# Attention scores in three fp32r passes, with ScalarE taking each head's exponentials and sums from PSUM

## The reference

```
h   = layer_norm(x);  qh = h @ wq + bq
kh  = ctx @ wk + bk, with one bias key appended;  vh = ctx @ wv + bv, with one bias value appended
w   = softmax(qh . kh / sqrt(128))          # 64 + 1 keys
x   = x + (w @ vh) @ wo + bo
```

## Time and profile before

| | |
|---|---|
| median of 3 runs | 1015.79 us (1015.21 to 1018.17) |
| profiled execution | 1017.42 us, span 1015.6 us, mean granted PE clock 0.982 |
| PE | 922.9 us busy, 91% of the span |
| PEld | 772.6 us, 76% |
| DVE | 615.3 us, 61% |
| ACT | 532.7 us, 52% |
| POOL | 485.1 us, 48% |
| chain that ended last | PE 74%, DVE 14%, ACT 5%, issue 4%, POOL 2% |

### The profile page before, as it was taken

One profiled execution on the slowest core, in us unless ns is written; L12 is line 12 of the kernel. 1 busy time (PEld: TensorE's weight loads), 2 busy tenths in 40 slices (PEclk: granted clock), 3 DMA queues, 4 the chain that ended last, 5 costly groups with the idle time before them and its releaser, 6 DMA issues.

```text
span 1015.6 us, 16288 instructions
## 1 busy us (share of the span) xinstructions
PE 922.9 (91%) x5784; PEld 772.6 (76%) x5784; DVE 615.3 (61%) x1380; ACT 532.7 (52%) x1300; POOL 485.1 (48%) x509
## 2 busy tenths in 40 slices
PE   5899989889998999989899899899998989989798
PEld 3677777789895678956689698799975679756698
DVE  2566758541778857789631465333779857788440
ACT  3777767654664326633455343664663336632662
POOL 2645657365453424545458144083544325455373
PEclk8999999999999999999999998899999999999999
DMA  9100000000362003310000200020460005200000
GB/s 343 42 1 2 2 1 2 1 2 1 125 217 85 1 1 125 126 63 1 1 21 2 83 2 1 2 93 22 152 253 1 1 22 164 65 1 0 2 11 32
DMA packets 15027, 52.49 MB, mean 52 GB/s; under 512 B 1507, under 2 KB 4067, under 8 KB 13796
## 3 DMA queue, kind: packets, MB, share of 16 engines
q1 hardware_dynamic: 14948, 51.46, 14.6%
HBM read 50.41 MB, written 1.05 MB: 51 GB/s over the span
## 4 chain that ended last, share of the span: by engine, by line
PE 74%; DVE 14%; ACT 5%; issue 4%; POOL 2%; DMA 0%; SPq 0%; DVEq 0%; ACTq 0%; POOLq 0%
PE ps L918 7%; PE ps L894 7%; PE ps L821 5%; PE ps L823 5%; PE ps L861 5%; PE ps L850 4%; PE ps L729 4%; PE ps L649 3%; PE ps L650 3%; PE ps L651 3%; PE ps L716 3%; PE ps L630 3%; PE ps L631 3%; PE ps L632 3%; PE ps L705 2%
## 5 line engine op out<-in xcount | busy, mean ns | idle before, releaser
L894 PE MATMUL ps<-arena,hT 128*128 128x512 f32 x256 | 120.0, 613 | 19.8 <-ACT hT L1247 19.8
L918 PE MATMUL ps<-arena,pT_all 128*128 128x256 f32 x512 | 116.4, 380 | 7.3 <-ACT pT_all L1306 5.9
L493 POOL TENSOR_TENSOR arena<-arena,rinv 128x640 f32<-128x640 f32 x64 | 80.5, 1258 | 83.9 <-DVE rinv L1447 83.9
L518 POOL TENSOR_TENSOR prob<-prob,rinv 128x512 f32<-128x512 f32 x32 | 49.5, 1548 | 133.8 <-DVE rinv L1643 133.8
L918 PEld LDWEIGHTS ps<-arena,pT_all 128*128 128x128 f32 x512 | 94.8, 190 | 20.6 <-ACT pT_all L1306 6.8
L485 POOL TENSOR_TENSOR rstd<-var,neg_half 128x1 f32<-128x1 f32 (+1 forms) x56 | 35.6, 635 | 154.9 <-DVE var L1462 154.9
L1313 ACT ACTIVATE prob<-prob 128x512 f32<-128x512 f32 x32 | 20.2, 631 | 162.0 <-DVE prob L1631 162.0
L894 PEld LDWEIGHTS ps<-arena,hT 128*128 128x128 f32 x256 | 48.6, 194 | 72.9 <-issue 48.2
L1199 ACT ACTIVATE arena_r<-ps,cols 128x256 fp32r<-128x256 f32 x128 | 66.6, 520 | 61.3 <-PE ps L632 61.3
L537 POOL TENSOR_TENSOR arena_r<-arena,arena_r 128x512 fp32r<-128x512 f32 x64 | 83.9, 1331 | 13.1 <-ACT arena L1200 13.1
L461 POOL TENSOR_TENSOR vacc<-vacc,vpart 128x256 f32<-128x256 f32 x60 | 44.1, 736 | 89.9 <-ACT vpart L1282 89.6
(11 more groups left out here) (164 smaller groups left out, 2451.5 us busy)
## 6 DMA issues: line engine op xcount, KB each, us to landing
ring<-in_heads_dram SPq DMA_DIRECT2D x64, 512.5 KB, 3.4
w<-in_w_dram SPq DMA_DIRECT2D x8, 1024.0 KB, 7.2
x<-in_x_dram SPq DMA_DIRECT2D x1, 1024.0 KB, 10.3
lnb<-in_lnb_dram SPq DMA_DIRECT2D x4, 256.0 KB, 8.8
ring<-in_wp_dram SPq DMA_DIRECT2D x1, 1024.0 KB, 5.3
out_dram<-x SPq DMA_DIRECT2D x4, 256.0 KB, 2.2
arena<-in_kinT_dram SPq DMA_DIRECT2D x1, 960.0 KB, 7.6
brow<-in_brow_dram SPq DMA_DIRECT2D x1, 768.0 KB, 11.5
```

Source lines behind the costliest of these rows:

```text
L493: g.tensor_tensor(w, w, rinv[:, n % 2, 0:2].unsqueeze(2).broadcast_to([P, 2, KEYS0]), ALU.mult)\
L894: last = mm(ps[:, half, :], hT[:, k, d, 0:P], A[:, d, b // 2, cols_of, sl, :].rearrange("p r s k -> p r (s k)"), start=(d == 0), stop=(d = ...
L918: last = mm(ps[:, 6, 0:D], pT[:, k, c, :], VW[:, b, c, :], start=(c == 0), stop=(c == PAIRS - 1))
```

## The change

In the wide attentions:

- Scores take three fp32r passes: twelve matmuls of 512 columns instead of four in fp32. The low part of A, `AL`, is made by DVE for each head in keys; the low part of h, `hL`, by DVE (`low`) for each tile. The score banks alternate, (0, 1) for even tiles and (2, 5) for odd ones.
- DVE only takes the maxima and scales them by -1/sqrt(128) (`largest`). ACT then makes, for each head by itself, exp(scale * score + neg) straight from PSUM into `prob`, with the sum of the 64 values as accumulator output (`exps`): sixteen ACTIVATEs of 128x64 a tile in place of two of 128x512. DVE's subtractions and sums go. What remains on DVE (bias key, reciprocal, normalisation of the second half) is `finish`.
- All of VW is copied by ACT.
- z, spread and power run one tile (z) and two tiles (spread, power) further ahead. constant_row moves ahead of the first scores. The MLP weights are split in tiles 4 to 7 only, the high parts by ACT, since `AL` of the first two batches lies in their place.
- Some tensor_scalar operations become tensor_tensor or scalar_tensor_tensor with a broadcast operand; memory is laid out anew; mask2 and kvd are made later; some MLP steps change place in their streams.

```diff
@@ TensorE, keys
                     if n >= 2:
-                        pe.wait_ge(a_act, n - 1)
+                        pe.wait_ge(a_low, n - 1)
...
-                    if h == 0:
+                    if h == 1:
                         turn_z(0, seq * TILES, bank=6)
+                    elif h == 2:
+                        turn_z(1, seq * TILES + 1)
@@ TensorE, tokens
                 def scores(g):
                     n, k, b = base + g, g % 2, g // 2
-                    pe.wait_ge(h_ready, n + 1)
-                    if g >= 1:
-                        pe.wait_ge(s_used, n)
+                    pe.wait_ge(hq_ready, TILES * a + g + 1)
+                    if g >= 2:
+                        pe.wait_ge(e_ready, n - 1)
                     sl = slice(2 * (b % 2), 2 * (b % 2) + 2)
                     for half in range(2):
+                        o = ps[:, SCORES[k][half], :]
                         cols_of = slice(4 * half, 4 * half + 4)
                         for d in range(DH):
-                            last = mm(ps[:, half, :], hT[:, k, d, 0:P],
-                                      A[:, d, b // 2, cols_of, sl, :].rearrange("p r s k -> p r (s k)"),
-                                      start=(d == 0), stop=(d == 1))
+                            aH = A[:, d, b // 2, cols_of, sl, :].rearrange("p r s k -> p r (s k)")
+                            aL = AL[b // 2][:, d, cols_of, sl, :].rearrange("p r s k -> p r (s k)")
+                            mm(o, hH[:, k, d, 0:P], aH, start=(d == 0), stop=False)
+                            mm(o, hH[:, k, d, 0:P], aL, start=False, stop=False)
+                            last = mm(o, hL[:, k, d, 0:P], aH, start=False, stop=(d == 1))
                         last.then_inc(s_half if half == 0 else s_ps, 1)
...
+                constant_row()
+                pe.wait_ge(a_low, H * (a + 1))
                 for i in range(TILES):
                     scores(i)
-                    if i == 0:
-                        constant_row()
-                    else:
+                    if i >= 1:
                         turn_p(i - 1)
-                    if i + 1 < TILES:
-                        turn_z(i + 1, base + i + 1)
-                    if a % 2 == 1 and i == TILES - 2:
+                    if i + 2 < TILES:
+                        pe.wait_ge(hq_ready, TILES * a + i + 2)
+                        turn_z(i + 2, base + i + 2)
+                    if a % 2 == 1 and i == TILES - 1:
+                        pe.wait_ge(hq_ready, TILES * (a + 1))
                         turn_m(a, 0)
-                    if i >= 2:
+                    if 2 <= i < TILES - 1:
                         output(i - 2)
-                if a % 2 == 1:
-                    pe.wait_ge(s_used, base + TILES)
+                if a % 2 == 0:
+                    output(TILES - 3)
+                    heads_kv(a + 1, 0)
+                    heads_kv(a + 1, 1)
+                    output(TILES - 2)
+                    turn_p(TILES - 1)
+                    output(TILES - 1)
+                else:
+                    output(TILES - 3)
                     up(a, 0, range(0, 4))
                     turn_m(a, 1)
-                output(TILES - 2)
-                if a % 2 == 0:
-                    pe.wait_ge(s_used, base + TILES)
-                    heads_kv(a + 1, 0)
-                    heads_kv(a + 1, 1)
-                else:
+                    output(TILES - 2)
+                    turn_p(TILES - 1)
                     up(a, 0, range(4, 6))
-                turn_p(TILES - 1)
-                output(TILES - 1)
-                if a % 2 == 1:
+                    output(TILES - 1)
                     up(a, 0, range(6, FT))
@@ ScalarE, keys
+                        a_(VW[0:C, h % 2:B:2, h // 2, :], ps[0:C, 4 + k, :].rearrange("p (g n) -> p g n", g=2), ACT.Copy)
                         a_(VW[C:P, 1 - h % 2:B:2, h // 2, :], ps[C:P, 4 + k, :].rearrange("p (g n) -> p g n", g=2),
                            ACT.Copy).then_inc(vw_act, 1)
@@ ScalarE, tokens
+                def exps(g, half):
+
+                    k = g % 2
+                    for h in range(half * H // 2, (half + 1) * H // 2):
+                        at = h % (H // 2) * C
+                        last = a_(prob[:, k, h * C:(h + 1) * C], ps[:, SCORES[k][half], at:at + C], ACT.Exp,
+                                  bias=neg[:, k, h:h + 1], scale=scale, accum_out=sm[:, k, h:h + 1])
+                    return last
+
                 for g in range(TILES):
                     n, k = base + g, g % 2
-                    act.wait_ge(sub_half, 8 * a + g + 1)
-                    a_(prob[:, k, 0:HALF], prob[:, k, 0:HALF], ACT.Exp, scale=scale).then_inc(e_half, 1)
+                    act.wait_ge(neg_first, 8 * a + g + 1)
+                    exps(g, 0)
                     if g >= 1:
                         turned_p(g - 1)
-                    act.wait_ge(s_used, n + 1)
-                    a_(prob[:, k, H * C:PN], mx2[:, k, :], ACT.Exp, scale=-scale)
-                    a_(prob[:, k, HALF:H * C], prob[:, k, HALF:H * C], ACT.Exp, scale=scale).then_inc(e_ready, 1)
-                    if g + 1 < TILES:
-                        plus_one(base + g + 1)
-                    if a % 2 == 1 and g == TILES - 2:
+                    act.wait_ge(neg_ready, 8 * a + g + 1)
+                    a_(prob[:, k, H * C:PN], neg[:, k, :], ACT.Exp)
+                    exps(g, 1).then_inc(e_ready, 1)
+                    if g + 2 < TILES:
+                        plus_one(base + g + 2)
+                    if a % 2 == 1 and g == TILES - 1:
                         turned_m(a, 0)
+                    if a % 2 == 1 and g >= TILES // 2:
+                        split_high(a, 2 * g - TILES)
+                        split_high(a, 2 * g - TILES + 1)
@@ VectorE, keys
-                    dve.wait_ge(vw_ps, n + 1)
-
-                    v.tensor_copy(VW[0:C, par:B:2, h // 2, :], ps[0:C, 4 + k, :].rearrange("p (g n) -> p g n", g=2))\
-                        .then_inc(vw_dve, 1)
+                    dve.wait_ge(a_act, n + 1)
+                    slots = slice(0, 4, 3) if par == 0 else slice(1, 3)
+                    for g in range(2):
+                        last = v.tensor_tensor(AL[g][:, :, h // 2, slots, :],
+                                               ps[:, 2 + k, :].rearrange("p (d g s k) -> p d g s k", d=DH, g=2, s=2)[:, :, g],
+                                               A[:, :, g, h // 2, slots, :].bitcast(F32), ALU.subtract)
+                    last.then_inc(a_low, 1)
+                    if h == 0:
+                        tile_z(f"T{a}", seq * TILES, 0)
+                        tile_z(f"T{a}", seq * TILES + 1, 1)
+                        tile_spread(2)
+                        tile_spread(3)
+                    elif h == 3:
+                        low(a, seq, 0)
+                        low(a, seq, 1)
@@ VectorE, tokens
                         link(v.tensor_reduce(mx[:, k, part[half]], main[half], AX.X, ALU.max))
-                        link(v.tensor_scalar(mx2[:, k, part[half]], mx[:, k, part[half]], 0.0, None, ALU.max))
-                        v.tensor_tensor(pm[half], main[half], of(mx2, half), ALU.subtract)\
-                            .then_inc(sub_half if half == 0 else s_used, 1)
...
+                        v.scalar_tensor_tensor(neg[:, k, part[half]], mx[:, k, part[half]], 0.0,
+                                               neg_scale[:, :].broadcast_to([P, H // 2]), ALU.max, ALU.mult)\
+                            .then_inc(neg_first if half == 0 else neg_ready, 1)
+
+                def finish(g):
+                    n, k = base + g, g % 2
+                    pm = prob[:, k, HALF:H * C].rearrange("p (h c) -> p h c", c=C)
                     dve.wait_ge(e_ready, n + 1)
-                    link(v.tensor_reduce(sm[:, k, part[1]], pm[1], AX.X, ALU.add))
                     link(v.tensor_tensor(sm[:, k, :], sm[:, k, :], prob[:, k, H * C:PN], ALU.add))
                     v.reciprocal(rinv[:, k, :], sm[:, k, :]).then_inc(rinv_ready, 1)
...
                 for g in range(TILES):
+                    if 1 <= g < TILES - 1:
+                        low(a, seq, g + 1)
                     if g + 2 < TILES:
-                        tile_spread(g + 2)
-                    if g + 1 < TILES:
-                        tile_z(f"T{a}", base + g + 1, g + 1)
+                        tile_z(f"T{a}", base + g + 2, g + 2)
+                    largest(g)
...
+                    if g + 4 < TILES:
+                        tile_spread(g + 4)
...
-                    softmax(g)
+                    finish(g)
                     if g >= 2:
                         add(g - 2)
```

More of the change, by code:

```diff
@@ L319, in build, with weight_part @@
         HALF = H // 2 * C
+        def weight_part(l, c):
+            part = slice(c % 2 * 512, c % 2 * 512 + 512)
+            two = slice(2 * (c - 4), 2 * (c - 4) + 2)
+            if c < 4:
```

(71 more changed lines are left out.)

163 lines of the change are left out of this document (85 added, 78 removed).

## The result

The changed kernel takes 1062.77 us (median of 4 runs, 1061.19 to 1064.82), the kernel before 1015.86 beside it: ratio 1.0462, 95% interval 1.0441 to 1.0483, slower. The forecast was 1046, in a range of 1030 to 1078. The profiled execution is 1063.46 us with a span of 1061.7, 46.1 more than before.

The account below looks back on a forecast made before the run. PE bounded the kernel before; after the change ACT and DVE taking turns would set the tile loop. 1015.6 + 29.2 (attentions) + 2 (keys) - 0.8 (start) = 1046 us, range 1030 to 1078.

Parts of the forecast that it names:

- ACT and DVE in turn: Tile loop: ACT's 6.01 us and DVE's 3.39 us alternate, a turn of 9.4 us against 8.0 before; chance 0.70.
- The exponential: Tile loop on ACT: each 64-column exponential with its sum costs 0.30 us, sixteen 4.8 us a tile.
- the dearer case: Rival in the tile loop: exponentials cost 0.34 to 0.40 us, time 1067 to 1096, about 1078; chance 0.13.
- PE's work: Tile loop: fp32r matmuls of 512 columns take 0.24 us, PE's work a tile 7.4 us, 0.6 less than before.
- Even attentions: T0 and T2: 85.0 us each against 76.5, the later scores(0) included.
- Head of an attention: Before the tile loop: constant_row waits for the last VW copy, so scores(0) starts 2.5 us later.
- Keys: Keys stage: z and spreads at h = 0 stall PE by 0.5 us an attention, +2 us in all.
- which hides that: Keys: DVE's 0.68 us standing a head covers two added subtractions of about 0.42 us, less a dropped copy of 0.68.
- PE stalls in keys: Keys: listed among the signs that would show the prediction wrong; no size given there.
- Odd attentions: T1 and T3: 89.6 us each against 83.5, with 15.6 us from e_ready(7) to the end of output(7).
- rival on PE's clock: Token loops: idle PE lowers the granted clock, deciding only if its mean is under 0.8; 1070 us, chance 0.06.
- MLPs and attend2 at nothing: Outside the wide attentions and keys: the MLPs, attend2 and the broadcast forms were costed at nothing.

Follow-up runs that it names:

- x2_noacc: The changed kernel with the sixteen exponentials a tile made without accumulator output, ones standing in for the sums: 1021.01 us, ratio 1.0039.
- x1_wide: The changed kernel with one 128x512 exponential for each half, without subtraction of the maxima and without sums: 992.64 us, ratio 0.9760.
- x8_pipe: The changed kernel with PE, ACT and DVE streams reordered together, all sixteen exponentials kept: 1013.09 us, ratio 0.9961.
- x4_fp32: The changed kernel with scores as four fp32 matmuls a tile instead of twelve fp32r, low-part products left out: 1068.32 us, ratio 1.0512.
- x5_keys: The changed kernel with z(0) and z(1) at heads 0 and 1 of keys and the spreads at head 2: 1066.80 us, ratio 1.0504.
- x10_keys: The changed kernel with z and spreads over heads 0 to 2 and POOL's powers of tiles 2 and 3 behind head 5: 1061.28 us, ratio 1.0419.
- x12_split: The changed kernel with POOL's low weight splits waiting for the next tile's maxima in T1 and T3: 1056.91 us, ratio 1.0389.
- x3_dveorder: The changed kernel with DVE taking the next tile's maxima directly behind finish, ahead of add, low and z: 1050.97 us, ratio 1.0321.
- x7_negts: The changed kernel with the maxima scaled by tensor_scalar with constants, one tensor operand instead of two: 1063.70 us, ratio 1.0447.
- x6_crow: The changed kernel with constant_row moved back behind scores(0): 1057.76 us, ratio 1.0397.

## Why the prediction was right, and where it was off

The mechanism was right. Of the 15.7 us that the sum lacks, most are two terms that were mis-sized: keys (1.8 us in each of four) and the tail of the odd attentions (2.1 in T1, read from its trace).

- **ACT and DVE in turn** (0.70, the forecast): shown. A turn of 9.16 us against 9.4, ACT's leg 5.95 against 6.01, DVE's 3.21 against 3.39. x2_noacc shortens ACT's leg by 1.46 us and the turn by the same, to 7.70; x1_wide shortens it further, until PE's 7.33 is the bound; x8_pipe takes DVE's leg off the loop, and the turn is 7.43 with all exponentials kept.
- **The exponential**, 0.30 us forecast, 0.29 measured, of which some 0.09 is the accumulator read. The row of 320 columns less its extra columns was the right neighbour. The Trainium skill's budget (ScalarE: Activation LUTs, Rules for kernel authors), 0.35 us here, is above the measured one: the dearer case didn't come.
- **PE's work**: 0.23 us for an fp32r matmul of 512 columns (0.24 forecast), 7.33 us a tile (7.4 forecast), with no part of it on the loop (x4_fp32).
- **Even attentions**: 82.05 us. The forecast had 82.5 behind its later scores(0), and no errors cancel in it: T0 is 7.6 us to the end of the first tile's exponentials, 63.3 for the seven turns and 11.1 of tail, against 7.6, 63.9 and 11.0.
- **Head of an attention**: 2.5 us forecast (its own terms, 309.2 less 306.8, make 2.4), 2.55 measured, and as it was told: 1.33 us until the last copy of VW, 1.22 for the row. What it left out is the wait for `AL`, 1.0 us, which lies under the row and shows only when the row is moved.
- **Keys**: mis-sized. 0.5 us of stall an attention forecast, 2.3 measured. The step that failed is "which hides that": I compared DVE's new work with a head's slack of 0.68 us in the steady state, but two z, two spreads and two low parts fall into the first four heads as well, and DVE has nothing left there. "PE stalls in keys" stood among the signs of being wrong, and they came (0.86 and 1.87 us). Moving the work to other heads doesn't help (x5_keys, x10_keys).
- **Odd attentions**: mis-sized, +3.6 each forecast, +6.5 and +5.8 measured. T1 is 7.6 us to the end of the first tile's exponentials, 64.8 for the turns and 17.7 of tail, against 7.6, 63.9 and 15.6. The turns are the collision of POOL's splits with DVE's small operation: 0.9 us over the forecast, 1.5 over the same turns of T0, and without it all of T1 is 2.7 us shorter (x12_split). The tail is the granted clock after a wait, in the windows and the timeline of the change:

```profile
519.00:523.90 4.90, 0.02 (x1) 0.00 (x0) 2.27 (x5) 4.90 (x22) 1.85 (x2) 0.80 0.00 0
523.90:527.00 3.10, 3.10 (x14) 3.10 (x15) 0.00 (x0) 1.55 (x3) 2.31 (x2) 0.50 0.00 0
```

```profile
524.28 0.41 PE L663 MATMUL ps<-hL,w1H 128*128 128x256 f32 x1
524.50 0.41 PE L664 MATMUL ps<-hH,w1L 128*128 128x256 f32 x1
```

  PE has no work for 4.88 us, until `mlp_split`; then the clock is 0.50, the lower of its two levels (1.2 GHz), and the 24 matmuls of the first four up blocks start 0.21 us apart instead of 0.12. They take 5.1 us where the sum had 2.9, and that is the tail's excess of 2.1. T3 has another 1.6 us over T1, 1.3 of them at its start: from scores(0) to the first exponential it takes 3.89 us, in T1 2.63, and the granted clock from 921.3 to 925.0 us is 0.54. My rival on PE's clock asked for a mean under 0.8 in the token loops; that was 0.96 in T0 and 0.89 in T1, so it didn't decide there. It cost its time in this tail and at the start of T3. No run took the clock's part by itself.
- **MLPs and attend2 at nothing**: attend2 holds (81.6 us from its first to its last matmuls, before and after). Of T1 to T2, 4.8 us are another keys as in the other rows; 1.4 remain there, 1.1 of them behind attend2, and 1.3 behind T3. No run looked for them.

## What to carry to other kernels

When work moves to another engine, draw the loop that the new waits close, across all streams, and sum its legs: here two engines at 65 and 54% busy made a turn that neither fills. Work that only feeds a later step (add, low, z) has to stand behind what the partner engine waits for, but every stream has to be moved together, or the wait comes back on another engine (x3_dveorder, x5_keys). Compare new work with the slack of the stretch that it lands in, not with that of the steady state.

## What was not expected of the hardware

- A DVE operation of 8 columns takes 0.17 us alone and 0.52 to 1.19 us while POOL runs a tensor_tensor of 512 columns on SBUF; the maxima just ahead of it, which read PSUM, keep their 0.68 us. In the last turn of T0 the same operation takes 0.64 us, beside POOL's addition of the constant row. In keys too, z takes 0.97 us instead of 0.48 beside POOL's work on vacc and u (x5_keys). I expected the form with one SBUF operand to escape, and it doesn't (x7_negts). The Trainium skill, SBUF — State Buffer, Who interferes with whom, says that VectorE and GpSimd share one pair of ports: a VectorE instruction with two SBUF inputs contends with a GpSimd instruction that reads SBUF, tensor_scalar can contend too where its operands allow a two-port mode, and tensor_reduce never does on trn2. The traces agree, with 0.79 us for the form with two inputs, 0.80 for tensor_scalar and 0.68 for the maxima; which mode the tensor_scalar ran in, no trace shows.
- An exponential of 64 columns is recorded with 0.31 to 0.42 us and its accumulator read with 0.19 to 0.32, growing along the row, while the starts stay 0.29 apart. Only the distance between starts is a cost.
- In keys of x6_crow, directly behind a stall of 1.84 us, the granted clock of one window is 0.66 and a head takes 5.07 us instead of 3.3; in the change the same stall is followed by a full clock. That ate what this run gained from T0 to T1.
